# Entry of the softmax attention: expert weight loads on the sync queue, constants filled in the second pipeline step, only some cells cleared

## The chip, the cores and the metric

The kernel runs on one core of a Trainium2 chip, in one launch. The core has five engines with their own instruction streams: TensorE (PE: matmuls, and PEld: its weight loads), VectorE (DVE), ScalarE (ACT), GpSimd (POOL) and SyncE (SP). [...] The metric is the device time of the launch in microseconds (us); lower is better. Before the change the three timed runs gave 1829.85, 1832.07 and 1848.2 us, a median of 1832.07 us.

## The reference, cut to what matters

A network of two layers works on 16 sequences of 256 tokens with 128 channels, float32. Each half layer is `x = x + f(layernorm(x))`:

```python
x = x + _L0_attn_ref(_layernorm(x), ...)   # linear recurrence
x = x + _L0_ffn_ref(_layernorm(x), ...)    # 32 experts, 4 per token
x = x + _L1_attn_ref(_layernorm(x), ...)   # squared-relu attention, 16 heads
x = x + _L1_ffn_ref(_layernorm(x), ...)    # softmax attention, then 8 experts, 1 per token
```

The change lies at the start of the last line. There `_L1_ffn_ref` computes

```python
hn = _layernorm(x, ln1_g, ln1_b)
q, k, v = hn @ wq + bq, hn @ wk + bk, hn @ wv + bv      # 16 heads of 8
attn = softmax(q k^T / sqrt(8)); x = x + (attn @ v @ wo + bo)
hn2 = _layernorm(x, ln2_g, ln2_b)
idx = argmax(hn2 @ gate_w + gate_b)                     # one of 8 experts
x = x + (relu(hn2 @ w1[idx] + b1[idx]) @ w2[idx] + b2[idx])
```

The weights `w1` and `w2` of the 8 experts (2 MB each) are what the change loads from another queue.

## The kernel before, in words

Every engine has its own program, written out by hand; the order of the work is the order of the lines, and engines meet only at semaphores. The program has five stages one after another: the recurrence (with the routing of the first experts), the 32 experts, the squared-relu attention, the softmax attention, and the 8 experts. Between the third and the fourth stage all engines meet at the semaphore `phases`, and SP and another engine clear semaphores for reuse (`cleared`). A printed order gives a reused semaphore the name of an earlier holder, so `x2T_made` in the rows of the change below is `set4`.

The fourth stage works sequence by sequence in a software pipeline of six parts, called `fetch`, `front`, `mid`, `att`, `tail` and `end`. In step n of the pipeline `fetch` treats sequence n+1, `front` sequence n, `mid` sequence n-1, and so on, so step 0 has only `fetch`, and step 1 has `fetch` of sequence 2 and `front` of sequence 1. The first nine steps are written out, then comes a loop. In each step every engine runs its own function `half`:

- `fetch`: SP loads the sequence's rows (`x3l`, 128 KB). DVE takes their moments (L1839 to L1842, `var4`), POOL turns them into an inverse deviation in some small steps (L714 to L755) and makes `x3n` (L756, L757), DVE makes `xn4` (L1845, L1846), PE transposes it (L1440), and ACT brings it from PSUM as `h4T` (L1024).
- `front`: PE multiplies `h4T` by the weights of q, k and v (L1398), DVE adds the biases and writes `v4` and `qk4` (L1875, L1877), and ACT and DVE split q and k into bf16 parts in the tile `terms4`. Its layout is 8 rows of 8 cells a head (`TERMS1`, `DH`); rows 0 to 5 are written in every step, cell 0 of row 6 is a maximum or the constant 1, and the other cells of rows 6 and 7 stay 0.
- `mid`, `att`, `tail`, `end`: the maxima of the scores, softmax and values, output projection with the next layernorm, and routing.

Before the pipeline starts, POOL sets the constants of the stage with memsets, which all add to the semaphore `set4`: `no_token` (L697), all of `terms4` and `v4` (two and four buffers), eight buffers `got` of the last stage, one row of `prior_b`, and then the ones in `terms4` and `v4` (L707, L709). DVE, ACT and PE each wait for all of them before their first instruction of the stage. ACT then starts five transfers, before its own `half`: the clearing of the table `token_dram` in memory, and the last stage's expert weights and biases `wa`, `wb`, `ba`, `bb` (L967, L970). `wa` and `wb` are 2 MB each. SP has the queue for the loads of `x3l` (L535), which it may run four sequences ahead: the load of sequence 5 waits for `kept_made` of sequence 1.

After the pipeline POOL waits for the last entries of the table to have landed, and for DVE's plan of the blocks (`plan_made`), then gathers the table's rows (L791) and the tokens of each block into `got` (L775).

Of the kernel before, what the change touches and what calls it, by code (L numbers as in the profile page):

```python
# [18 lines left out]
P = 128  # L19
# [12 lines left out]
DH = 8  # L32
# [6 lines left out]
AHEAD = 8  # L39
# [36 lines left out]
def pipeline(eng, half, stages=4, unroll=2):  # L76

    def step(turn, at):  # L80
        work = [Seq(turn, at - lag, unroll) if not isinstance(turn, int) or 0 <= at - lag < BATCH else None
                for lag in range(stages)]
        half(*work)


    lead = stages - 1
    turns = (BATCH - lead) // unroll
    for at in range(lead + unroll):
        step(0, at)
    with eng.Fori(1, turns) as turn:  # L90
        for place in range(unroll):
            step(turn, lead + place)
    for at in range(lead + unroll * turns, BATCH + lead):
        step(0, at)
# [20 lines left out]
def build_program(nc, a, out):  # L115
    with ExitStack() as ctx:
# [32 lines left out]
        token_dram = dram("token_dram", (NO_ROWS + P, 1), U32)  # L149
# [104 lines left out]
        s = {}  # L254
# [82 lines left out]
        for name in ("x2_made qk_squared qk_copied v_squared v_copied "  # L337
# [1 line left out]
                     "score_ps relu_made attn_made attn_made_pool attn_made_act attn_read aggr_out aggr_sq_made nsq_ps o_norm_made o_len_made "  # L339
                     "o_tanh_made o_factor_made fT_ps fT_made F_ps gated o_made y3_ps x3_made yg_cleared phases cleared").split():  # L340
            s[name] = sem(name)
        N_SET = 14 + AHEAD
        ring = [bank[6], bank[7]]
        G_BANK = (0, 0, 1, 1)
        FT_BANK = (1, 0)
# [23 lines left out]
        v4 = four("v4", [P, 2, HEADS, COLS])  # L369
# [75 lines left out]
        def _(sp):  # L445
# [69 lines left out]
            def half(fetch, front, att, tail, end):  # L515
                if fetch:
                    wait(sp, s["x2_made"], fetch.n - 2)
                    sp.dma_start(x1l[fetch.p][:], rows(x1_dram, (fetch.n - 1) * SEQ, SEQ, 2)).then_inc(s["x1l_landed"][fetch.p], 16)
                    sp.dma_start(routel[fetch.p][:], rows(route_dram, (fetch.n - 1) * SEQ, SEQ, 2)).then_inc(s["routel_landed"][fetch.p], 16)
                if end:  # L520
                    sp.wait_ge(s["x3_made"], end.n)
                    sp.dma_start(rows(x3_dram, (end.n - 1) * SEQ, SEQ, 2), x3[end.p][:]).then_inc(s["x3_stored"][end.p], 16)
# [7 lines left out]
                sp.sem_clear(semaphore)  # L530
            sp.sem_inc(s["cleared"], 1)
            def half(fetch, front, mid, att, tail, end):
                if fetch:
                    wait(sp, s["kept_made"], fetch.n - 4)
                    sp.dma_start(x3l[fetch.q][:], rows(x3_dram, (fetch.n - 1) * SEQ, SEQ, 2)).then_inc(s["x3l_landed"][fetch.q], 16)  # L535
                if tail:
                    sp.wait_ge(s["x4n_made"], tail.n)
                    sp.wait_ge(s["sum_made"], tail.n)
                    sp.dma_start(rows(x4n_dram, (tail.n - 1) * SEQ, SEQ, 2), x4n[tail.p][:]).then_inc(s["x4_stored"][tail.p], 16)
# [6 lines left out]
        def _(pool):  # L546
# [148 lines left out]
            no_more = pool.to_reg(NO_ROWS - 1)  # L695
            last_token = pool.to_reg(TOK - 1)
            pool.memset(no_token[:], TOK).then_inc(s["set4"], 1)  # L697
            for p in range(2):
                pool.memset(terms4[p][:], 0.0).then_inc(s["set4"], 1)
            for p in range(4):  # L700
                pool.memset(v4[p][:], 0.0).then_inc(s["set4"], 1)
            for n in range(AHEAD):
                pool.memset(got[n][:], 0.0).then_inc(s["set4"], 1)
            pool.memset(prior_b[:, 0:1, :], 0.0).then_inc(s["set4"], 1)
            pool.wait_ge(s["set4"], 8 + AHEAD)
            for p in range(2):
                pool.memset(terms4[p][:, 1, :, :, 6, 0:1].rearrange("q j h a -> q (j h) a"), 1.0).then_inc(s["set4"], 1)  # L707
            for p in range(4):
                pool.memset(v4[p][:, :, :, DH:DH + 1], 1.0).then_inc(s["set4"], 1)  # L709
            pool.wait_ge(s["set4"], N_SET)  # L710

            def inverse_deviation(var, meanvar_x, veps_x, rstd_x, done, count):
                hold(s[var], count)
# [2 lines left out]
                pool.tensor_tensor(rstd_x[:], veps_x[:], minus_half[:, 0:2], ALU.pow).then_inc(s[done], 1)  # L716

            def half(fetch, front, mid, att, tail, end):
                if att:
                    if not isinstance(att.n, int) or att.n > 2:  # L720
                        hold(s["x4_made"], att.n - 2)
                    if not isinstance(att.n, int) or att.n > 2:
                        hold(s["sum_made"], att.n - 2)
                    pool.tensor_copy(x3_plain[att.p][:], x3l[att.q][:]).then_inc(s["plain_made"], 1)
                    hold(s["x3n_made"], att.n)
                    pool.tensor_tensor(x3_kept[att.p][:], x3n[att.q][:], b_o[:].unsqueeze(1).to_broadcast([P, 2, D]), ALU.add).then_inc(s["kept_made"], 1)
                if tail:
                    inverse_deviation("var5", meanvar5, veps5, rstd5, "rstd5", tail.n)
                if end:
                    hold(s["slot1_made"], end.n)  # L730
                    pool.wait_ge(s["table_cleared"], 16)
                    for j in range(2):
                        pool.indirect_dma_start(
                            token_dram, bass.IndirectOffsetOnAxis(ap=slot_b[end.p][:, j:j + 1], axis=0),
                            token[end.p][:, j:j + 1], None, bounds_check=no_more, oob_is_err=False,
                        ).then_inc(s["token_sent"][end.p], 16)
                if tail:
                    if not isinstance(tail.k, int) or tail.k > 1:
                        hold(s["x4_stored"][tail.p], 16 * (tail.k - 1))
                    hold(s["plain_made"], tail.n)  # L740
                    pool.tensor_tensor(x4n[tail.p][:, :, 0:D], x4[tail.p][:], x3_plain[tail.p][:], ALU.add).then_inc(s["sum_made"], 1)
                if fetch:


                    inverse_deviation("var4", meanvar4, veps4, rstd4_in, "rstd4_in", fetch.n)
                    hold(s["rstd4_in"], fetch.n)
                    n = chain.step(pool.tensor_tensor(veps4[:], rstd4_in[:], rstd4_in[:], ALU.mult))
                    chain.need(n)
                    n = chain.step(pool.tensor_tensor(veps4[:], veps4[:], meanvar4[:, :, 1], ALU.mult))
                    chain.need(n)  # L750
                    n = chain.step(pool.tensor_scalar(veps4[:], veps4[:], 1.0, LN_EPS, ALU.mult, ALU.add))
                    chain.need(n)
                    n = chain.step(pool.tensor_tensor(rstd4_norm[:], veps4[:], minus_half[:, 0:2], ALU.pow))
                    chain.need(n)
                    pool.tensor_tensor(rstd4[:], rstd4_norm[:], rstd4_in[:], ALU.mult).then_inc(s["rstd4"], 1)  # L755
                    chain.step(pool.tensor_scalar(x3n[fetch.q][:, 0, :], x3l[fetch.q][:, 0, :], meanvar4[:, 0, 0:1], rstd4_in[:, 0:1], ALU.subtract, ALU.mult))  # L756
                    pool.tensor_scalar(x3n[fetch.q][:, 1, :], x3l[fetch.q][:, 1, :], meanvar4[:, 1, 0:1], rstd4_in[:, 1:2], ALU.subtract, ALU.mult).then_inc(s["x3n_made"], 1)  # L757
                if fetch or tail:
                    chain.restart()

            pipeline(pool, half, 6, 4)
            for p in range(2):
                pool.wait_ge(s["x4_stored"][p], 16 * BATCH // 2)

            def rows_for(dst, turn, q):

# [43 lines left out]
        def _(act):  # L810
# [151 lines left out]
            act.wait_ge(s["phases"], 10)  # L962
            act.wait_ge(s["cleared"], 2)
            act.wait_ge(weights_in, 16 * N_WEIGHT_DMA)
            act.wait_ge(s["set4"], N_SET)

            act.dma_start(token_dram.rearrange("(q n) a -> q (n a)", q=P), no_token[:]).then_inc(s["table_cleared"], 16)  # L967
            for dst, src in ((wa[:], a["wa"].rearrange("e q f -> q e f")), (wb[:], a["wb"].rearrange("e (c q) d -> q (e c) d", q=P)),
                             (ba[:], a["ba"]), (bb[:], a["bb"])):
                act.dma_start(dst, src).then_inc(s["experts_in"], 16)  # L970

            def exp(att, head):
                wait(act, s["pv_made"], HEADS * (att.n - 1) + head + 1 - 4)
# [11 lines left out]
                act.activation(dst[:, 4 * c:4 * c + 4, :].rearrange("q a t -> q (a t)"), ring[x].bitcast(BF16), ACT.Copy).then_inc(s[what + "_out"], 1)  # L985

            def half(fetch, front, mid, att, tail, end):
                flat = terms4[front.p][:].rearrange("q w j h m d -> q (w j h) m d") if front else None
                qk_flat = qk4[:].rearrange("q w j (h d) -> q (w j h) d", d=DH)
                for g in range(PAIRS):  # L990
# [63 lines left out]
        def _(pe):  # L1054
# [241 lines left out]
            pe.drain().then_inc(s["phases"], 1)  # L1296
            pe.wait_ge(s["phases"], 10)
            pe.wait_ge(s["cleared"], 2)
            pe.wait_ge(s["set4"], N_SET)
            readers = [[], []]  # L1300
            LAST_USER = (15, 13, 14)

# [63 lines left out]
                mm.then_inc(s[what + "_ps"], 1)  # L1366

            def half(fetch, front, mid, att, tail, end):

                if end:  # L1370
                    readers[0] = [(s["h5T_made"], end.n)]
# [116 lines left out]
        def _(dve):  # L1488
# [340 lines left out]
            dve.wait_ge(s["phases"], 10)  # L1829
            dve.wait_ge(s["cleared"], 2)  # L1830
            dve.wait_ge(weights_in, 16 * N_WEIGHT_DMA)
            dve.wait_ge(s["set4"], N_SET)
            n = chain.step(dve.tensor_copy(token_f[:], token_start[:]))
            chain.need(n)
            chain.restart()
# [28 lines left out]
                    dve.tensor_reduce(heads[:, :, jp, :], psum[:, 4:6, :].rearrange("q a (b k) -> q a b k", b=2), AX, ALU.max, negate=True).then_inc(s["max_made"], 1)  # L1864

            def half(fetch, front, mid, att, tail, end):
                for g in range(PAIRS):
                    if mid:
                        take_maxima(mid, g)
# [233 lines left out]
```

## Time and profile before

| | us |
|---|---|
| median of the 3 runs shown | 1832.07 |
| the profiled execution | 1849.76 |
| its span on the core | 1848.1 |
| PE / DVE / ACT / POOL busy | 1281.9 / 1097.8 / 755.9 / 902.4 |
| last piece of the third stage (DVE `x3`, L1807) starts | 1178.12 |
| first instruction of the fourth stage (SP, load of `x3l`) | 1180.94 |

The profile's page is of one execution on the chip; times inside it count from its first instruction. A timeline row gives start, duration, engine, line of the kernel, operation, tiles and how many of them (x4), and in square brackets how long the engine had been idle and what released it. Queues (ACTq, SPq, POOLq) are the instruction streams that start transfers: their duration is that of the issue and not of the transfer. In tables by stretch PEclk is TensorE's granted clock as a share of full speed: 0.50 is 1.2 GHz, and 1.00 is 2.4 GHz. The DMA share is the mean busy share of the 16 DMA engines.

### The profile page before, as it was taken

How to read it: one execution, taken by the hardware profiler on the slowest of the kernel's cores; microseconds unless marked ns; L12 is line 12 of the kernel's file. 1: busy time of each engine (PE TensorE's matmuls, PEld its weight loads, DVE VectorE, ACT ScalarE, POOL GpSimd, SP SyncE). 2: the span in 40 equal slices, each digit the busy share in tenths (PEclk: the TensorE clock that was granted, in tenths of full speed). 3: DMA queues.
4: the chain of work that ended last, by engine and by line, in shares of the span. 5: the costliest groups of instructions: out<-in, count | busy, mean ns of one | idle time of the engine just before them, and what ended most of it. 6: DMA issues, size and time to landing. Idle time of an engine off the chain costs nothing. (4 is left out here: it accounts for less than half of the span.)

```text
span 1848.1 us, 26758 instructions
## 1 busy us (share of the span) xinstructions
PE 1281.9 (69%) x8186; PEld 770.1 (42%) x8187; DVE 1097.8 (59%) x2712; ACT 755.9 (41%) x1238; POOL 902.4 (49%) x1119
## 2 busy tenths in 40 slices
PE   3434331636788888888788888348888887847796
PEld 1222221413455555545455555324443443426685
DVE  7777771156666666666666653157787777743232
ACT  1101100315555555555555554026666665632221
POOL 2355567543566666666566644512332332225554
PEclk7555555667788888789788777559999988978766
DMA  4000001700000000000000000120000000001110
GB/s 135 22 15 26 14 2 37 143 16 5 2 8 8 7 7 8 7 7 7 8 7 7 4 4 4 43 72 10 18 11 18 18 18 10 13 19 46 40 42 11
DMA packets 73600, 41.61 MB, mean 23 GB/s; under 512 B 23979, under 2 KB 68908, under 8 KB 73476
## 3 DMA queue, kind: packets, MB, share of 16 engines
q1 hardware_dynamic: 50674, 24.02, 4.8%
q0 software_dynamic: 20432, 11.70, 3.1%
q10 hardware_dynamic: 2370, 4.35, 0.8%
q8 instruction: 65, 1.06, 0.3%
q14 instruction: 59, 0.48, 0.1%
HBM read 31.16 MB, written 23.87 MB: 30 GB/s over the span
## 5 line engine op out<-in xcount | busy, mean ns | idle before, releaser
L1864 DVE TENSOR_REDUCE terms<-psum 128x4 bf16<-128x1024 f32 x128 | 156.9, 1226 | 47.4 <-PE psum L1356 36.9
L1173 PE MATMUL psum<-attn,v 128*64 128x256 f32 x1024 | 163.9, 448 | 1.6 <-ACT aggT L886 1.6
L862 ACT ACTIVATE attn<-psum 128x1024 f32<-128x1024 f32 x128 | 130.5, 1019 | 81.7 <-PE psum L1160 81.5
L632 POOL TENSOR_TENSOR o_inv<-o_norm,minus_half 128x16 f32<-128x16 f32 x32 | 93.3, 2917 | 136.6 <-DVE o_norm L1688 136.6
L975 ACT ACTIVATE prob<-psum 128x512 f32<-128x512 f32 x256 | 138.7, 596 | 38.4 <-PE psum L1320 37.8
L623 POOL DMA_INDIRECT yg<-ye_dram,routel x128 | 131.6, 1028 | 45.1 <-issue 39.0
L714 POOL TENSOR_SCALAR veps<-meanvar 128x2 f32<-128x2 f32 x32 | 6.2, 193 | 294.5 <-DVE meanvar L1842 293.5
L576 POOL DMA_INDIRECT xe_dram<-rows_out,route x128 | 130.4, 1019 | 39.7 <-issue 39.1
L1333 PE MATMUL psum<-prob,v 128*32 128x256 f32 x1024 | 144.6, 406 | 0.7 <-ACT pvT L980 0.4
L1189 PE MATMUL psum<-x3T,w_g 128*128 128x256 f32 x256 | 77.7, 431 | 35.0 <-DVE silu_g L1702 20.1
L1683 DVE TENSOR_TENSOR attn<-psum,attn 128x1024 f32<-128x1024 f32 x80 | 97.0, 1212 | 6.1 <-ACT attn L862 3.1
L1173 PEld LDWEIGHTS psum<-attn,v 128*64 128x64 f32 x1024 | 69.6, 153 | 70.3 <-issue 35.6
L1253 PE MATMUL psum<-w_out,oT 128*128 128x128 f32 x512 | 87.0, 349 | 3.5 <-POOL oT L656 3.5
L1253 PEld LDWEIGHTS psum<-w_out,oT 128*128 128x128 f32 x512 | 84.0, 261 | 8.3 <-issue 8.3
L876 ACT ACTIVATE tanh_g<-psum 128x512 f32<-128x512 f32 x64 | 38.0, 593 | 114.1 <-PE psum L1189 114.1
L1198 PEld LDWEIGHTS psum<-pair_sum,agg_sq 128*128 128x128 f32 x512 | 77.1, 235 | 9.6 <-DVE kT L1713 6.9
L1160 PE MATMUL psum<-qT,kT 64*128 64x256 f16 x512 | 56.9, 305 | 33.1 <-DVE attn L1683 29.0
L1198 PE MATMUL psum<-pair_sum,agg_sq 128*128 128x2 f32 x512 | 77.2, 281 | 2.8 <-DVE kT L1713 1.9
L1356 PE MATMUL psum<-k_highT,q_highT 32*128 32x256 bf16 x512 | 53.9, 291 | 36.4 <-DVE terms L1864 35.5
L656 POOL TENSOR_TENSOR oT<-gate,aggT 128x1024 f32<-128x1024 f32 x32 | 75.5, 2358 | 5.6 <-remote 4.3
L1189 PEld LDWEIGHTS psum<-x3T,w_g 128*128 128x128 f32 x256 | 48.5, 205 | 68.4 <-issue 34.6
L1223 PE MATMUL psum<-ident,terms 128*128 128x128 f16 x512 | 54.1, 280 | 31.9 <-DVEq L1760 31.2
(308 smaller groups left out, 3050.7 us busy)
## 6 DMA issues: line engine op xcount, KB each, us to landing
x4n_dram<-x4n SPq DMA_DIRECT2D x16, 256.0 KB
w<-in_w POOLq DMA_DIRECT2D x48, 64.0 KB, 2.6
x_in<-in_x SPq DMA_DIRECT2D x8, 256.0 KB, 2.7
xe_dram<-zero_rows SPq DMA_DIRECT2D x8, 256.0 KB, 3.0
x_dram<-x1s SPq DMA_DIRECT2D x8, 256.0 KB
xe_dram<-rows_out,route POOLq DMA_INDIRECT x128
xe<-xe_dram SPq DMA_DIRECT2D x16, 128.0 KB
ye_dram<-ye SPq DMA_DIRECT2D x16, 128.0 KB, 2.2
```

Of the source, the lines that this page charges most:

```text
L576: pool.indirect_dma_start(xe_dram, bass.IndirectOffsetOnAxis(ap=where[:, j, K0 + k:K0 + k + 1], axis=0), rows_out[p][:, j, :], None, bound ...
L623: pool.indirect_dma_start(yg[fetch.p][:, j, k, :], None, ye_dram, bass.IndirectOffsetOnAxis(ap=where[:, j, K0 + k:K0 + k + 1], axis=0), bo ...
L632: n = chain.step(pool.tensor_tensor(o_inv[:], o_norm[:], minus_half[:].rearrange("q (j h) -> q j h", j=2), ALU.pow))
L862: act.activation(r[:], psum[:, 2 * (g % 2):2 * (g % 2) + 2, :], ACT.Relu).then_inc(s["relu_made"], 1)
L975: act.activation(prob[head % 4][:], bank[head % 3][:], ACT.Exp, scale=SCALE).then_inc(s["exp_made"], 1)
L1173: mm = pe.matmul(bank[4 + g % 4 // 2][DV * h:DV * h + DV, g % 2 * SEQ:(g % 2 + 1) * SEQ], v[q.p][:, c, head * DV:(head + 1) * DV], attn[g ...
L1189: mm = pe.matmul(b[:, c * SEQ:(c + 1) * SEQ], w_g[:, (2 * u + c) * P:(2 * u + c + 1) * P], x3T[:], start=True, stop=True)
L1198: mm = pe.matmul(b[:, HALF * j + 2 * c:HALF * j + 2 * c + 2], agg_sq[:, c, j * P:(j + 1) * P], pair_sum[:], start=True, stop=True)
L1253: mm = pe.matmul(b[:, j * D:(j + 1) * D], oT[:, c, j * P:(j + 1) * P], w_out[:, c, :], start=(c == 0), stop=(c == PAIRS - 1))
L1333: mm = pe.matmul(bank[3][part, t * SEQ:(t + 1) * SEQ], v4[q.q][:, c, head, :], prob[head % 4][:, c * SEQ:(c + 1) * SEQ], start=(c == 0), s ...
L1683: dve.tensor_tensor(r[:], psum[:, 2 * (g % 2):2 * (g % 2) + 2, :], r[:], ALU.mult).then_inc(s["attn_made"], 1)
L1864: dve.tensor_reduce(heads[:, :, jp, :], psum[:, 4:6, :].rearrange("q a (b k) -> q a b k", b=2), AX, ALU.max, negate=True).then_inc(s["max_ ...
```

## The change: what it does

Four edits, all about the entry of the fourth stage:

1. The transfers of `token_dram` and of the four expert tensors are issued by SP instead of ACT: the table is cleared ahead of the load of sequence 2, as soon as `no_token` is set, and the weights and biases go out ahead of the load of sequence 5.
2. POOL sets only `no_token` before the pipeline. The memsets of `v4`, `terms4` and `prior_b` and the ones stand at the start of POOL's second step.
3. DVE, ACT and PE wait for `set4` at the start of their second step instead of ahead of the first.
4. Of `terms4` only rows 6 and 7 of each head are cleared (128x1024 cells instead of 128x4096, in each of the two buffers), and `got` is cleared after the pipeline, with a wait of POOL for it in front of the last stage.

```diff
@@ SP
             def half(fetch, front, mid, att, tail, end):
+                if fetch and isinstance(fetch.n, int) and fetch.n == 5:
+                    for dst, src in ((wa[:], a["wa"].rearrange("e q f -> q e f")), (wb[:], a["wb"].rearrange("e (c q) d -> q (e c) d", q=P)),
+                                     (ba[:], a["ba"]), (bb[:], a["bb"])):
+                        sp.dma_start(dst, src).then_inc(s["experts_in"], 16)
+                if fetch and isinstance(fetch.n, int) and fetch.n == 2:
+                    sp.wait_ge(s["set4"], 1)
+                    sp.dma_start(token_dram.rearrange("(q n) a -> q (n a)", q=P), no_token[:]).then_inc(s["table_cleared"], 16)
                 if fetch:
                     wait(sp, s["kept_made"], fetch.n - 4)
@@ POOL
             pool.memset(no_token[:], TOK).then_inc(s["set4"], 1)
-            for p in range(2):
-                pool.memset(terms4[p][:], 0.0).then_inc(s["set4"], 1)
-            for p in range(4):
-                pool.memset(v4[p][:], 0.0).then_inc(s["set4"], 1)
-            for n in range(AHEAD):
-                pool.memset(got[n][:], 0.0).then_inc(s["set4"], 1)
-            pool.memset(prior_b[:, 0:1, :], 0.0).then_inc(s["set4"], 1)
-            pool.wait_ge(s["set4"], 8 + AHEAD)
...
+            def set_constant_parts():
+                for p in range(4):
+                    pool.memset(v4[p][:], 0.0).then_inc(s["set4"], 1)
+                for p in range(2):
+                    pool.memset(terms4[p][:, :, :, :, 6:8, :].rearrange("q w j h m d -> q (w j h) (m d)"), 0.0).then_inc(s["set4"], 1)
+                pool.memset(prior_b[:, 0:1, :], 0.0).then_inc(s["set4"], 1)
+                pool.wait_ge(s["set4"], 8)
...
+                pool.wait_ge(s["set4"], N_SET)
...
             def half(fetch, front, mid, att, tail, end):
+                if front and isinstance(front.n, int) and front.n == 1:
+                    set_constant_parts()
...
             pipeline(pool, half, 6, 4)
+            for n in range(AHEAD):
+                pool.memset(got[n][:], 0.0).then_inc(s["set4"], 1)
             for p in range(2):
                 pool.wait_ge(s["x4_stored"][p], 16 * BATCH // 2)
+            pool.wait_ge(s["set4"], N_SET + AHEAD)
@@ ACT (the same wait moves on PE and DVE)
-            act.wait_ge(s["set4"], N_SET)
-
-            act.dma_start(token_dram.rearrange("(q n) a -> q (n a)", q=P), no_token[:]).then_inc(s["table_cleared"], 16)
-            for dst, src in ((wa[:], a["wa"].rearrange("e q f -> q e f")), (wb[:], a["wb"].rearrange("e (c q) d -> q (e c) d", q=P)),
-                             (ba[:], a["ba"]), (bb[:], a["bb"])):
-                act.dma_start(dst, src).then_inc(s["experts_in"], 16)
...
             def half(fetch, front, mid, att, tail, end):
+                if front and isinstance(front.n, int) and front.n == 1:
+                    act.wait_ge(s["set4"], N_SET)
```

The order on POOL, from the end of the third stage, before the change:

```order
L656 TENSOR_TENSOR oT<-gate,aggT 128x1024 [waits gated,y3_ps]
L63 ISA [waits pool_chain]
L697 MEMSET no_token 128x257 [waits cleared,phases]
L699 MEMSET terms 128x4096 x2
L701 MEMSET v 128x1024 x4
L703 MEMSET got 128x256 x8
L704 MEMSET prior_b 128x8
L707 MEMSET terms 128x32 [waits x2T_made]
L707 MEMSET terms 128x32
L709 MEMSET v 128x32 x4
L714 TENSOR_SCALAR veps<-meanvar 128x2 [waits x2T_made,var4]
L716 TENSOR_TENSOR rstd_in<-veps,minus_half 128x2 [waits pool_chain]
```

And in the changed kernel, up to the same place in step 1:

```order
L704 MEMSET no_token 128x257 [waits cleared,phases]
L722 TENSOR_SCALAR veps<-meanvar 128x2 [waits var4]
...
L766 TENSOR_SCALAR x3n<-x3l,meanvar,rstd_in 128x128
L767 TENSOR_SCALAR x3n<-x3l,meanvar,rstd_in 128x128
L63 ISA [waits pool_chain]
L709 MEMSET v 128x1024 x4
L711 MEMSET terms 128x64x16 x2
L712 MEMSET prior_b 128x8
L715 MEMSET terms 128x32 [waits x2T_made]
L715 MEMSET terms 128x32
L717 MEMSET v 128x32 x4
L722 TENSOR_SCALAR veps<-meanvar 128x2 [waits x2T_made,var4]
```

The whole `fetch` of sequence 1 now stands between `no_token` and the other memsets, `got` has left this place, and the memsets of `terms4` are narrower.

SP's queue at the entry of the stage, in the changed kernel (before, the four loads of `x3l` stood there alone, and the next one waited for `kept_made`):

```order
L542 DMA x3l<-x_dram 128x2x128
L539 DMA token_dram<-no_token 128x257 [waits x2T_made]
L542 DMA x3l<-x_dram 128x2x128 x3
L536 DMA wa<-in_wa 128x8x512
L536 DMA wb<-in_wb 128x32x128
L536 DMA ba<-in_ba 128x32
L536 DMA bb<-in_bb 1x1024
L542 DMA x3l<-x_dram 128x2x128 [waits kept_made]
```

The five transfers stand between loads of `x3l`, all of them ahead of the first one that waits for the pipeline.

## Rows read from the trace of the kernel before

**Rows 1.** Timeline of POOL at the entry: start, duration, engine, line, operation [idle before]

```profile
1181.13 0.31 POOL L697 MEMSET no_token<- 128x257 uint32 x1 [9.35 <-SPq L530]
1181.38 6.96 POOL L699 MEMSET terms<- 128x4096 bf16 x2
1188.28 3.64 POOL L701 MEMSET v<- 128x1024 f32 x4
1191.86 2.10 POOL L703 MEMSET got<- 128x256 f32 x8
...
1194.17 0.48 POOL L709 MEMSET v<- 128x32 f32 x4
...
1199.88 0.78 POOL L757 TENSOR_SCALAR x3n<-x3l,meanvar,rstd_in 128x128 f32<-128x128 f32 x1
```

**Rows 2.** Timeline of ACT and its queue, same stretch, same columns

```profile
1194.76 0.37 ACTq L967 DMA_DIRECT2D token_dram<-no_token  x1
...
1196.81 11.56 ACTq L970 DMA_DIRECT2D ba<-in_ba  x1
...
1209.00 0.56 ACT L1024 ACTIVATE h4T<-psum,norms 128x256 f32<-128x256 f32 x1 [13.11 <-issue]
```

**Rows 3.** Timeline of DVE and PE, same stretch, same columns

```profile
1195.16 0.49 DVE L1839 BATCH_NORM_STATS2 stats<-x3l 128x6 f32<-128x128 f32 x2 [0.20 <-DVE token_f L1833]
...
1199.51 0.45 DVE L1846 TENSOR_SCALAR xn<-x3l,meanvar,rstd 128x128 f32<-128x128 f32 x1
...
1200.11 0.66 PE L1440 MATMUL psum<-ident,xn 128*128 128x128 f32 x2 [22.08 <-DVE xn L1846]
...
1209.71 2.90 PE L1398 MATMUL psum<-w_qkv,h4T 128*128 128x384 f32 x4 [8.94 <-ACT h4T L1024]
```

**Rows 4.** Transfers by issue: tiles, count, KB each, median us from issue to landing

```profile
x1l<-x_dram SPq DMA_DIRECT2D x16, 128.0 KB, 2.2
```

**Rows 5.** Timeline of SP's queue: the first loads, and that of sequence 5

```profile
1180.94 62.59 SPq L535 DMA_DIRECT2D x3l<-x_dram  x5
...
1243.15 0.37 SPq L535 DMA_DIRECT2D x3l<-x_dram  x1
```

**Rows 6.** Stretches of 2 us: length, ACT busy (x), PEclk, DMA share, GB/s

```profile
1183.00:1185.00 2.00, 0.00 (x0) 0.50 0.55 147
...
1201.00:1203.00 2.00, 0.00 (x0) 0.50 1.05 402
...
1209.00:1211.00 2.00, 0.56 (x1) 0.50 1.03 279
```

**Rows 7.** The page's DMA queues: packets, MB, share of 16 engines

```profile
q8 instruction: 65, 1.06, 0.3%
```

**Rows 8.** Timeline of POOL and DVE between pipeline and last stage

```profile
1653.21 0.97 POOL L733 DMA_INDIRECT token_dram<-token,slot_b  x1 [0.30 <-issue]
...
1657.63 0.15 DVE L1996 TENSOR_SCALAR block_at_i<-block_at 128x1 uint32<-128x1 f32 x1
1660.95 1.05 POOL L791 DMA_INDIRECT block_tokens<-token_dram,block_at_i  x1 [6.77 <-DMA token_dram<-token,slot_b]
```

**Rows 9.** Stretches of 5 us: length, PE busy (x), PEclk, DMA share, GB/s

```profile
1140.00:1145.00 5.00, 5.00 (x27) 0.50 0.01 2
...
1235.00:1240.00 5.00, 4.13 (x34) 0.50 0.02 3
1240.00:1245.00 5.00, 4.49 (x22) 0.50 0.09 26
1245.00:1250.00 5.00, 4.84 (x46) 1.00 0.00 0
```

**Rows 10.** POOL's first instruction of two steps in the loop

```profile
1329.57 0.19 POOL L714 TENSOR_SCALAR veps<-meanvar 128x2 f32<-128x2 f32 x1 [14.77 <-DVE meanvar L1842]
1354.30 0.19 POOL L714 TENSOR_SCALAR veps<-meanvar 128x2 f32<-128x2 f32 x1 [14.58 <-DVE meanvar L1842]
```

**Rows 11.** A stretch of 50 us: length, PE, PEld, DVE, ACT, POOL busy (x), PEclk, DMA share, GB/s

```profile
1400.00:1450.00 50.00, 41.68 (x388) 19.97 (x384) 39.60 (x112) 32.84 (x57) 17.63 (x32) 1.00 0.08 17
```

More of the change, by code:

```diff
@@ L341, in build_program @@
             s[name] = sem(name)
-        N_SET = 14 + AHEAD
+        N_SET = 14
         ring = [bank[6], bank[7]]
@@ L697, in _ @@
             pool.memset(no_token[:], TOK).then_inc(s["set4"], 1)
-            for p in range(2):
-                pool.memset(terms4[p][:], 0.0).then_inc(s["set4"], 1)
-            for p in range(4):
-                pool.memset(v4[p][:], 0.0).then_inc(s["set4"], 1)
-            for n in range(AHEAD):
-                pool.memset(got[n][:], 0.0).then_inc(s["set4"], 1)
-            pool.memset(prior_b[:, 0:1, :], 0.0).then_inc(s["set4"], 1)
-            pool.wait_ge(s["set4"], 8 + AHEAD)
[L706 to L710, printed above, removed]
+            def set_constant_parts():
[5 more added lines that the diff above has]
+                pool.wait_ge(s["set4"], 8)
+                for p in range(2):
+                    pool.memset(terms4[p][:, 1, :, :, 6, 0:1].rearrange("q j h a -> q (j h) a"), 1.0).then_inc(s["set4"], 1)
+                for p in range(4):
+                    pool.memset(v4[p][:, :, :, DH:DH + 1], 1.0).then_inc(s["set4"], 1)
+                pool.wait_ge(s["set4"], N_SET)
             def inverse_deviation(var, meanvar_x, veps_x, rstd_x, done, count):
@@ L1298, in _ @@
             pe.wait_ge(s["cleared"], 2)
-            pe.wait_ge(s["set4"], N_SET)
             readers = [[], []]
@@ L1368, in half @@
             def half(fetch, front, mid, att, tail, end):
+                if front and isinstance(front.n, int) and front.n == 1:
+                    pe.wait_ge(s["set4"], N_SET)
                 if end:
@@ L1831, in _ @@
             dve.wait_ge(weights_in, 16 * N_WEIGHT_DMA)
-            dve.wait_ge(s["set4"], N_SET)
             n = chain.step(dve.tensor_copy(token_f[:], token_start[:]))
@@ L1866, in half @@
             def half(fetch, front, mid, att, tail, end):
+                if front and isinstance(front.n, int) and front.n == 1:
+                    dve.wait_ge(s["set4"], N_SET)
                 for g in range(PAIRS):
```

## The prediction

> **What bounds the kernel now.** The change touches one place, so I read the profile from that place outward, not from the busy shares. First the timelines of all engines from the end of the third stage to the first steps of the fourth. SP issues the first load of `x3l` at 1180.94 us [rows 5], and TensorE's first multiplication of a sequence's `front` starts at 1209.71 [rows 3]. In these 28.8 us TensorE does two transposes. So this stretch is pure entry, and whatever shortens it moves all that follows, if nothing behind it is bound by something that stays where it is.
>
> Two blocks fill it. POOL sets constants from 1181.13 to 1194.65 (start of the first memset; 1194.17 + 0.48, end of the last) [rows 1], and DVE takes its first moments only then, at 1195.16 [rows 3], although the rows it reads have long been there: a load of this size lands 2.2 us after its issue [rows 4], and the traffic of the four first loads is seen up to 1185 [rows 6]. Then `fetch` of sequence 1 runs quickly, and its transposes end at 1200.77 (1200.11 + 0.66) [rows 3]. But ACT copies them only at 1209.00: its queue had been held for 11.56 us in the issue of the small load `ba`, which stands behind the 4 MB of `wa` and `wb` [rows 2], while the DMA engines were full (share 1.05) from about 1195 to 1211 [rows 6]. That second block costs 8.1 us, from 1200.9 to 1209.0.
>
> **The change, part by part.** All against the profiled execution.
>
> *Waits moved to step 1, memsets behind `fetch` of sequence 1.* DVE can start when `x3l` lands, 1180.94 + 2.2 = 1183.1; with the semaphore about 1183.2. POOL is free then: `no_token` takes 0.31 us [rows 1]. From DVE's first moments to POOL's last `x3n` took 1200.66 - 1195.16 = 5.50 us (1199.88 + 0.78 is the end) [rows 1, 3], so POOL starts its memsets at 1188.7. The same stretch gives the transposes: 1200.77 - 1195.16 = 5.6 us, so they end at 1188.8.
>
> *The weights leave ACT.* ACT is then free for `h4T` at 1188.9, and 0.7 us later (1209.00 to 1209.71 [rows 2, 3]) TensorE could multiply, at 1189.6. At SP the same hold of 11.6 us is free of charge: behind it stands the load of sequence 5, which waited for `kept_made` until 1243.15 in any case [rows 5]; about 15 us earlier that is 1228, and SP would be free near 1198. The loads of sequences 2 to 4 are issued ahead of the weights; only the small clearing of the table (issue 0.37 us [rows 2]) stands between them and the first.
>
> Here a rule speaks against this edit. The row shows an issue of 11.56 us on the queue of a busy engine [rows 2]. The Trainium skill (DMA: Bandwidth & Descriptors, "Issuing engines are not separate DMA queues") says that the queues of all engines end on the same 16 DMA engines, so that another issuing engine saves only the time of the initiation, usually small beside the transfer. By it the edit would bring next to nothing, and the sum would be 8.1 us smaller, 6.7. The trace agrees with the sharing and disagrees with "small", and I go by the row.
>
> *The memsets that are left.* `v4` 3.6 us (1188.28 to 1191.86); `terms4` a quarter of the cells, 6.96 / 4 = 1.74 us; `prior_b` and the ones, from the end of `got` to the end of the last, 1194.65 - 1193.96 = 0.7 us, with the wait between them [rows 1]. Together 6.1 us. No row shows a memset of 128x64x16 cells in strides. It could not cost less than its cells, and I bound it above by the whole tile's 6.96 us, 5.2 more than I take. I take the cells, since `terms4` (4096 cells in 3.48 us) and `v4` (1024 in 0.9) agree on 0.85 ns a cell whatever the tile. So `set4` is complete at 1188.7 + 6.1 = 1194.8, and TensorE starts at 1194.9. This is 5.3 us later than 1189.6: **POOL's memsets, not the matmul's input, end last in the new entry.** The wait is at the head of step 1 on DVE, ACT and PE; nothing else is queued behind it that could have run, since step 1 begins with `front`, and the loads go on by themselves.
>
> *`got` cleared at the end.* 2.1 us [rows 1], between the last scatter of the table's entries (ends 1654.18) and the gather at 1660.95. POOL idles 6.77 us there, waiting for the scatter to land, and DVE's plan is ready at 1657.8 [rows 8]. So it costs nothing; were the landing itself held up by it, 2.1 us.
>
> *Three waits and the order elsewhere*: no price. The `fetch` of sequence 2 hangs on DVE in step 1, and everything from there on is shifted as a block.
>
> Sum: 1209.71 - 1194.9 = **14.8 us** less. The profiled execution would go from 1849.76 to 1835.0 us. It lies 17.7 us above the median of the runs shown, so against that median, 1832.07 - 14.8 = **1817.3 us**, a ratio of 0.992. The bounds of the sum are 9.6 us (strided memset as dear as the whole tile) and 20.1 us (memsets hidden altogether, 1189.6).
>
> **How far a gain of this size can be told.** The shown times spread over 18 us: two near 1831, one at 1848.2, and the profiled one with 1849.76. Something outside the entry moves this kernel by 1%, more than this change does. I call within 1% what a measurement can't tell from no change.
>
> **The rivals.**
>
> *TensorE's clock rises earlier.* The granted clock is 0.50 (1.2 GHz) all through the entry and steps 1 to 3 and rises at about 1245, after stretches with PE busy 4.13 and 4.49 us of 5 [rows 9]. A shorter gap might let it rise a step or two sooner. The q, k, v multiplication takes 2.90 us at the low level [rows 3]; halved, and with transposes and maxima in proportion, some 5 us could go on top: 1812. Against it: steps 1 and 2 are short of work for TensorE whatever precedes them, and 17 us of idle still stand ahead. The Trainium skill (TensorE: Matmul & The Clock Gate, "HAM oscillation") holds that waits between groups of matmuls send the engine back to its low level, so that each group begins slowly; by it nothing would be gained here, and the time stays 1817. The trace agrees as far as it goes: 0.50 in every sparse stretch. Chance 0.15.
>
> *The new step 1 is held up on the way in*: by a dearer strided memset, or by instructions that arrive late. Instructions come over the same DMA engines (65 transfers in one such queue [rows 7]), the weights now fill these from about 1184 to 1200, and step 1 runs from 1194.9 in the midst of that; before, the engines mostly waited then. If an engine had to wait until the burst ends, that is 5 us, as much as the dear memset: 1822.5. The Trainium skill (Runtime: NRT & Kernel Launch, "Instruction fetch mechanics") says that instruction streams are refilled in blocks by DMA while the present block runs, and mostly hidden; by that the time is the forecast's. Before, nothing is seen to be late in the burst (transposes 0.15 us behind their input [rows 3]). Chance 0.13.
>
> *The clock stays low (slower).* At 1140 TensorE was busy for all of 5 us and still granted only 0.50 [rows 9], so much work does not always bring the high level. In the loop a step takes 24.7 us (1329.57 to 1354.30 [rows 10]) with PE busy 83% at full clock [rows 11]: 20.6 us, which would be 41 at half, so each step at the low level costs up to 16.5 us. The place is steps 3 onward, whose start falls elsewhere in time than before. One such step eats the gain, two end at 1850, 1.0% slower. For it speaks only the spread; against it that the rise came promptly at 1245. Chance 0.08, of which 0.05 slower by over 1%.
>
> *The change doesn't do what it says*: the first `x3l` lands late, because the table or the weights go ahead of it, and the entry stays as it was, 1832. The order has it first on the queue. Chance 0.04.
>
> **Chances and range.** The forecast has 0.60. Its ratio of 0.992 is 3.5 us short of the 1% line at 1813.7, and the spread of runs is larger: I give 0.11 of it to faster by over 1%, 0.01 to slower, 0.48 to within. With the early clock (0.14 faster, 0.01 same), the held-up step (0.13 same), the low clock (0.05 slower, 0.03 same) and no effect (0.04 same): faster 0.25, same 0.69, slower 0.06. The range reaches from 1810 (the bound of 20.1 us less 2 us of spread) to 1836 (a gain of 14.8 us on the upper group of times, 1848.2 to 1849.8, is 1833.4 to 1835.0).
>
> **What would show it.** In the profile of the changed kernel: DVE's first moments about 2.2 us behind SP's first load; the ACT row of `h4T` 5 to 6 us later with no issue on ACTq; POOL's memsets for some 6 us right behind `x3n`, `terms` with 0.87 us each; TensorE's first q, k, v multiplication 14 us after that first load and released by POOL; a long issue of `ba` on SPq that nobody waits for; the gather L791's counterpart still released by the landing of the table's entries; the rise of the clock some 35 us behind the first multiplication, as before. Wrong would be the sum if that multiplication starts at the right place and the time is not lower: then the loss lies in the clock or behind step 1.

## The result

The changed kernel took 1822.7 us in the median of 8 runs, beside 1841.12 us for the kernel before (8 runs, the three shown at the top among them). The ratio is 0.9897, 95% interval 0.9849 to 0.9946: 19 us less, with 10 to 28 us possible. Timed a second time on another occasion it was 0.991 (0.9874 to 0.9945), 1824.07 against 1838.05 us, where the medians alone give 14.0 us and 0.992. Ratios and intervals are estimated from the single runs, without two slow executions of the kernel before, so they differ a little from the quotients of the medians. The entry of the fourth stage became 15.0 us shorter in the profile, where 14.8 had been worked out. That is 0.992 of the whole and lies inside both intervals.

The profiled execution of the changed kernel had a span of 1816.5 us, 31.6 less than before. Only 15.0 us of that lie in the entry, as the stretches show (starts of the same instructions in both profiles; what the other 9.1 and 7.9 us are worth is told with the second profile of the kernel before, below):

| stretch | before | changed | less |
|---|---|---|---|
| start to first load of the second stage | 314.98 | 305.91 | 9.1 |
| second and third stage | 865.96 | 866.18 | -0.2 |
| **entry: SP's first `x3l` to the first q, k, v multiplication** | **28.77** | **13.78** | **15.0** |
| from there to the gather of the table | 451.24 | 443.36 | 7.9 |
| from there to the end | 187.2 | 187.3 | -0.1 |

### The profile page after: what moved, and what is told of

It is laid out like the page before. It is cut to its first block and busy times, and to the rows that moved or that the text cites. A ratio compares the mean times of both kernels' runs of the same rounds, so it can differ in the third digit from the quotient of the medians.

```text
span 1816.5 us, 26759 instructions
## 1 busy us (share of the span) xinstructions
PE 1267.4 (70%) x8186; PEld 758.0 (42%) x8187; DVE 1097.8 (60%) x2712; ACT 756.0 (42%) x1237; POOL 898.0 (49%) x1119
```

## The profile after

The timeline of the changed kernel at the entry, POOL first. The columns are those of [rows 1]; these rows answer to them.

```profile
1172.29 0.31 POOL L704 MEMSET no_token<- 128x257 uint32 x1 [9.37 <-SPq L530]
...
1178.99 0.78 POOL L767 TENSOR_SCALAR x3n<-x3l,meanvar,rstd_in 128x128 f32<-128x128 f32 x1
1179.72 3.61 POOL L709 MEMSET v<- 128x1024 f32 x4
1183.29 1.83 POOL L711 MEMSET terms<- 128x1024 bf16 x2
...
1185.34 0.48 POOL L717 MEMSET v<- 128x32 f32 x4
```

The memsets run one behind the other from 1179.72 to 1185.82, 6.10 us, right behind `x3n`. The two strided ones of `terms4` take 1.83 us together, where the whole tiles took 6.96 [rows 1].

SP's queue and the other engines in the same stretch, which answer to [rows 2, 3, 5]:

```profile
1172.09 0.39 SPq L542 DMA_DIRECT2D x3l<-x_dram  x1
1172.63 0.36 SPq L539 DMA_DIRECT2D token_dram<-no_token  x1
...
1174.26 0.49 DVE L1848 BATCH_NORM_STATS2 stats<-x3l 128x6 f32<-128x128 f32 x2 [1.98 <-DMA x3l<-x_dram]
...
1176.15 11.11 SPq L536 DMA_DIRECT2D ba<-in_ba  x1
...
1179.21 0.66 PE L1450 MATMUL psum<-ident,xn 128*128 128x128 f32 x2 [10.02 <-DVE xn L1855]
...
1179.99 0.56 ACT L1033 ACTIVATE h4T<-psum,norms 128x256 f32<-128x256 f32 x1 [22.54 <-PE psum L1450]
...
1185.87 2.93 PE L1408 MATMUL psum<-w_qkv,h4T 128*128 128x384 f32 x4 [6.00 <-POOL v L717]
```

Read the brackets. DVE's moments are now released by the landing of `x3l`, 2.17 us after its issue, and no longer by a memset. ACT's `h4T` follows the transposes (0.12 us behind their end) and is released by them, where 13.11 us of idle had ended in "issue" [rows 2]. And the multiplication is released by POOL's last memset of `v`, after 6.00 us of idle. The long issue of `ba` is still there with 11.11 us, but on a queue that nobody waits for: SP's next load goes out at 1219.38, 32 us after that issue ends.

TensorE's clock, in the form of [rows 9]:

```profile
1185.00:1190.00 5.00, 2.93 (x4) 0.50 1.03 281
...
1215.00:1220.00 5.00, 4.35 (x27) 0.50 0.00 0
1220.00:1225.00 5.00, 4.99 (x32) 0.75 0.09 26
1225.00:1230.00 5.00, 3.81 (x38) 1.00 0.00 0
```

The high level comes at about 1222, 36 us behind the first multiplication; before it was 35 (1245 against 1209.71). The first of these rows also shows the multiplication running inside the burst of the weights (DMA share 1.03): it takes 2.93 us there. Before it took 2.90 [rows 3], in the last 2 us of the burst [rows 6], and in a kernel without a burst at this place (`late_weights`, below) 2.92.

The place of the `got` memsets, in the form of [rows 8]:

```profile
1620.94 0.97 POOL L743 DMA_INDIRECT token_dram<-token,slot_b  x1 [0.30 <-issue]
1621.90 2.10 POOL L773 MEMSET got<- 128x256 f32 x8
1629.23 1.05 POOL L804 DMA_INDIRECT block_tokens<-token_dram,block_at_i  x1 [5.23 <-DMA token_dram<-token,slot_b]
```

POOL still idles behind them, for 5.23 us, until the table's entries have landed.

## Experiments

"Landmark" is the entry as in the table above, 28.77 us before and 13.78 in the changed kernel.

### Edit 1 alone

```diff
@@ kernel before
-            act.dma_start(token_dram..., no_token[:])...
-            for dst, src in ((wa[:], ...), (wb[:], ...), (ba[:], ...), (bb[:], ...)):
-                act.dma_start(dst, src).then_inc(s["experts_in"], 16)
@@ SP, half: as in the change (table ahead of sequence 2, weights ahead of sequence 5)
```

> The kernel before with edit 1 alone: the table's clearing and the expert weights go out on SP, all memsets stay in front as they were. Landmark: from SP's first load of x3l to the start of TensorE's first q, k, v multiplication (28.8 us before, 13.8 in the changed kernel). Theory (ACT's queue was held by the issue behind the 4 MB): h4T follows the transposes at once, the landmark falls by 8.1 to about 20.7 us, the time by 8 us. Rival (by the Trainium skill, DMA: Bandwidth & Descriptors, "Issuing engines are not separate DMA queues", only the initiation is saved): landmark 28, time unchanged. Second rival (the transfer itself, not its issue, held ACT's first copy up): landmark 28 too.

Measured: landmark 20.65 us, ratio 0.9938 (0.9912 to 0.9964). Its timeline:

```profile
1174.55 0.39 SPq L542 DMA_DIRECT2D x3l<-x_dram  x1
...
1178.61 10.95 SPq L536 DMA_DIRECT2D ba<-in_ba  x1
...
1194.49 0.56 ACT L1027 ACTIVATE h4T<-psum,norms 128x256 f32<-128x256 f32 x1 [34.58 <-PE psum L1443]
1195.20 2.90 PE L1401 MATMUL psum<-w_qkv,h4T 128*128 128x384 f32 x4 [0.83 <-ACT h4T L1027]
```

`h4T` is released by the transposes, and the landmark falls by 8.1 us as expected; the interval of the ratio leaves out the rival's "time unchanged". The transfers are the same; what went is ACT's hold in the issue. The second rival, that the transfer itself held up ACT's first copy, isn't refuted by this run alone, since here the DMA engines had fallen idle by 1193, ahead of `h4T`. The changed kernel refutes it: its `h4T` at 1179.99 runs in the middle of the burst (DMA share 1.05 from 1180 to 1185) and follows the transposes by 0.12 us. So what the Trainium skill (DMA: Bandwidth & Descriptors, "Issuing engines are not separate DMA queues") says, that another issuing engine saves only the initiation, holds; its "usually small" does not hold behind 4 MB, where the issue takes 11 to 12 us.

### Everything but edit 1

```diff
@@ changed kernel, SP: the five dma_start taken out again
@@ ACT
             act.wait_ge(weights_in, 16 * N_WEIGHT_DMA)
+            act.wait_ge(s["set4"], 1)
+            act.dma_start(token_dram..., no_token[:])...    # and wa, wb, ba, bb as before
```

> The changed kernel with edit 1 undone: memsets moved, narrowed and split as in the change, but ACT still issues the table's clearing (after no_token) and the four expert tensors ahead of its first step. If the edits added up, this would be worth 15.0 - 8.1 = 6.9 us: landmark 21.9. Theory (the two blocks overlap once the memsets are out of the way, each hides most of the other): ACT's hold runs from about 1 us to 14 us after SP's first load, h4T starts near 14.3, multiplication near 15: landmark 15, time 13.8 us below before. So edit 1 would be worth only about 1.2 us of the changed kernel.

Measured: landmark 16.42 us, ratio 0.9919 (0.9882 to 0.9955).

```profile
1168.40 2.00 SPq L535 DMA_DIRECT2D x3l<-x_dram  x4
...
1171.06 12.42 ACTq L976 DMA_DIRECT2D ba<-in_ba  x1
...
1181.64 0.48 POOL L710 MEMSET v<- 128x32 f32 x4
...
1184.11 0.56 ACT L1032 ACTIVATE h4T<-psum,norms 128x256 f32<-128x256 f32 x1 [13.97 <-issue]
1184.82 2.90 PE L1407 MATMUL psum<-w_qkv,h4T 128*128 128x384 f32 x4 [8.64 <-ACT h4T L1032]
```

The theory of overlap holds: edits 2 to 4 alone bring 12.35 us and not 6.9, since ACT's hold now runs while `x3l` lands, `fetch` is worked on and POOL clears. I was 1.4 us short: the issue of `ba` ends 15.1 us after the first load, not 14 (it took 12.42 us here). So edit 1 is worth 8.1 us on the old entry and 2.6 us (16.42 - 13.78) on the new one, where I had expected 1.2.

### The whole of `terms4` cleared

```diff
@@ changed kernel, POOL
-                    pool.memset(terms4[p][:, :, :, :, 6:8, :].rearrange(...), 0.0)
+                    pool.memset(terms4[p][:], 0.0)
```

> The changed kernel with the whole of terms4 cleared (128x4096 cells in each of two buffers instead of 128x1024). Theory (POOL's memsets end last in the new entry): they take 5.2 us longer (6.96 instead of 1.83 us), and the landmark grows by the same, from 13.8 to 18.9. Rival (the matmul's input or the weights' transfer ends last): landmark stays below 15.

Measured, in a single run: landmark 18.77 us.

```profile
1186.06 6.96 POOL L711 MEMSET terms<- 128x4096 bf16 x2
...
1193.77 2.93 PE L1408 MATMUL psum<-w_qkv,h4T 128*128 128x384 f32 x4 [11.12 <-POOL v L717]
```

The memsets took 5.13 us longer and the multiplication started 4.99 us later, with the same releaser. POOL's memsets are what ends last. Without the narrowing the change would have taken 10.0 us from the entry (28.77 to 18.77), with it 15.0.

### The memsets split once more

```diff
@@ changed kernel, POOL: step 0, ahead of the first moments
+                if not front and fetch:
+                    set_first_parts()      # v4[0], terms4[0], prior_b and their ones
@@ POOL: step 1
-                    set_constant_parts()
+                    set_other_parts()      # v4[1..3], terms4[1], got and their ones
@@ PE, ACT, DVE
-                if front and isinstance(front.n, int) and front.n == 1:
-                    pe.wait_ge(s["set4"], N_SET)
+                if front and isinstance(front.n, int) and front.n < 3:
+                    pe.wait_ge(s["set4"], 6 if front.n == 1 else N_SET + AHEAD)
```

> The changed kernel with the memsets split again: what step 1 reads (v4, terms4 of sequence 1, prior_b) is set ahead of the first moments, while x3l lands and POOL idles 2.6 us; the other three v4, the other terms4 and got are set in step 1 and waited for in step 2. Theory (POOL's memsets end last, the input only 5.3 us earlier): the landmark falls from 13.8 to 8.5 us, the time by another 5.3 us, to 20 us below before; and with got out of the place after the pipeline, the table's entries land about 0.5 us earlier after the last scatter (7.3 us in the changed kernel, 6.8 before). Rival (something else is just behind, as the weights' transfer): landmark 12 or more.

Measured: landmark 8.57 us, ratio 0.9862 (0.9825 to 0.9899).

```profile
1175.96 0.95 POOL L711 MEMSET terms<- 128x1024 bf16 x1
1176.76 0.49 DVE L1864 BATCH_NORM_STATS2 stats<-x3l 128x6 f32<-128x128 f32 x2 [1.95 <-DMA x3l<-x_dram]
...
1177.73 0.19 POOL L739 TENSOR_SCALAR veps<-meanvar 128x2 f32<-128x2 f32 x1 [0.42 <-DVE meanvar L1867]
...
1182.48 0.56 ACT L1049 ACTIVATE h4T<-psum,norms 128x256 f32<-128x256 f32 x1 [22.50 <-PE psum L1466]
...
1183.19 2.90 PE L1424 MATMUL psum<-w_qkv,h4T 128*128 128x384 f32 x4 [0.83 <-POOL v L709]
```

The first memsets, 1024 cells of `v4` and of `terms4` and the small ones, fit into the time in which `x3l` lands, and POOL still waits 0.42 us for the moments. The multiplication starts 0.71 us after `h4T`, as before in [rows 2, 3]. The releaser named there, a memset of `v`, had not been on the way: it belongs to the count that is waited for one step later. The second expectation failed in part: from the start of the table's last scatter to the gather it took 8.21 us, against 8.29 with `got` in between. With `got` in that place five profiles gave 7.94 to 8.29 us; without it seven gave 7.72 to 8.64, two of them of the kernel before. The memsets there cost nothing that shows.

### The kernel before against itself

> The kernel before, unchanged, against itself, to see how much of the measured difference can be chance. Every kernel timed so far came out 3 to 5 us further below before than its entry is shorter (w_only 11.4 against 8.1, m_only 14.9 against 12.4, the changed kernel 18.9 against 15.0, early_fills 25.4 against 20.2). In the profiles the first load of the second stage (xe) starts at 314.98 us before and at 305 to 306 in all five others, though the first stage's code is the same. Theory (chance, of the first stage's own): ratio within 0.3% of 1, and xe at either value. Rival (something of the program before slows its first stage in every execution): xe near 315 again, and a first stage that costs the changed kernel's lead some us which the change's description doesn't hold.

Measured: ratio 0.999 (0.9955 to 1.0025). The first load of the second stage starts at 305.88 us, and the landmark is 28.66.

```profile
1165.14 1.93 SPq L535 DMA_DIRECT2D x3l<-x_dram  x4
...
1193.80 2.90 PE L1398 MATMUL psum<-w_qkv,h4T 128*128 128x384 f32 x4 [8.84 <-ACT h4T L1024]
```

So the 9.1 us of the first stage in the table above are chance of one execution (the other eleven profiles have 304.2 to 306.2 us there), and the landmark repeats within 0.1 us. Of the 7.9 us between the entry and the gather most is chance too: this second profile of the kernel before takes 445.04 us there, the first took 451.24, and the ten profiles of changed kernels 440.3 to 445.3. The ratio's interval, 0.35% to either side, says how much chance can do in the times: 6 us. The third stage shows where most of the spread of the times is: the stretch from 365 us to the first `x3l`, in this execution and in the first one of the changed kernel (length, busy time of PE, PEld, DVE, ACT and POOL, PEclk, DMA share, GB/s):

```profile
365.00:1165.14 800.14, 628.44 (x3744) 377.62 (x3744) 496.35 (x992) 404.78 (x544) 458.79 (x445) 0.83 0.03 7
```

```profile
365.00:1172.09 807.09, 640.60 (x3744) 384.06 (x3744) 496.83 (x992) 405.50 (x544) 456.82 (x444) 0.81 0.03 7
```

The busy times of DVE and ACT agree to 0.2%; the length goes with TensorE's granted clock. Over the twelve profiles of this study it was 800 to 824 us at mean clocks of 0.83 down to 0.78, in a stage that no kernel here changes.

### The weights four steps later

```diff
@@ changed kernel, SP
-                if fetch and isinstance(fetch.n, int) and fetch.n == 5:
+                if fetch and isinstance(fetch.n, int) and fetch.n == 9:
```

> The changed kernel with the four expert tensors issued by SP ahead of the load of sequence 9 instead of 5, so that the entry runs without their 4 MB on the DMA engines. Theory (the transfer doesn't hold up the new step 1): landmark from SP's first load to the first q, k, v multiplication 13.8 us as in the changed kernel, and from there to the first store of x4n 76.4 us within 1. Rival (step 1 is held up by the burst, through late instructions or data): both together shorter by 2 us or more.

Measured, in a single run: landmark 13.85 us, and 74.95 us from there to the first store of `x4n` (76.44 in the changed kernel).

```profile
1182.10 0.39 SPq L542 DMA_DIRECT2D x3l<-x_dram  x1
...
1195.95 2.92 PE L1408 MATMUL psum<-w_qkv,h4T 128*128 128x384 f32 x4 [6.01 <-POOL v L717]
```

```profile
1195.00:1200.00 5.00, 2.92 (x4) 0.50 0.00 0
```

The DMA engines are idle now (share 0.00), and the landmark and the multiplication are as with the burst. The second stretch is 1.5 us shorter, outside the "within 1" of the theory and short of the rival's 2 us. But a second profile of the changed kernel (below), with the burst in its place, shows 74.95 too, and `early_fills`, whose first multiplication starts some 9 us before its burst ends, took 76.31 and 73.17 in its two profiles. So this stretch moves by more than 1.5 us from one execution to the next, and nothing shows that the burst holds up step 1.

### TensorE kept busy through the entry

```diff
@@ early_fills, PE
+            def keep_busy(count):
+                for _ in range(count):
+                    pe.matmul(bank[2][:, 0:P], before[:], ident_b[:], start=True, stop=True)
+            keep_busy(70)
...
+                    if front and not att and isinstance(front.n, int):
+                        keep_busy((20 if g == 0 else 80 if g == 2 else 0) if front.n == 1 else 10)
```

> early_fills with extra bf16 matmuls 128x128 on TensorE, whose result nobody reads (70 ahead of the first transposes of the stage, 80 + 20 in step 1, 10 in each eighth of step 2), to keep it busy through the entry. This prices the rival of the earlier clock. Theory (the low clock of steps 1 to 3 costs a few us, and work brings the high level): granted clock 1.00 from step 1 on, and from the first q, k, v multiplication to the first store of x4n about 71 us instead of 76.3; time 5 us below early_fills. Rival (the steps are bound by DVE and ACT, so the clock is worth nothing there, or the extra matmuls don't raise it): 76 us or more.

Measured: from the first multiplication to the first store 71.37 us, against 76.31 in `early_fills`; ratio 0.9897 (0.9849 to 0.9945).

```profile
1170.63 6.88 PE L1330 MATMUL psum<-ident_b,before 128*128 128x128 bf16 x70 [2.97 <-SPq L530]
...
1178.74 1.53 PE L1431 MATMUL psum<-w_qkv,h4T 128*128 128x384 f32 x4 [0.83 <-ACT h4T L1049]
```

```profile
1175.00:1180.00 5.00, 4.17 (x37) 0.84 0.92 303
1180.00:1185.00 5.00, 4.59 (x79) 1.00 1.05 330
1185.00:1190.00 5.00, 1.64 (x30) 1.00 0.78 213
```

The clock rises inside the entry, the q, k, v multiplication takes 1.53 instead of 2.90 us, and 4.9 us go from the profile. But the high level doesn't stay, as the theory had it. After the last row, in which TensorE was busy for 1.64 of 5 us, it is gone again, and the multiplication of sequence 2 takes its 2.90 us:

```profile
1190.00:1195.00 5.00, 4.29 (x14) 0.52 0.00 0
```

```profile
1191.91 2.90 PE L1431 MATMUL psum<-w_qkv,h4T 128*128 128x384 f32 x4 [0.21 <-ACT h4T L1049]
```

In the times the gain wasn't to be seen (`early_fills` had 0.9862), so three kernels were timed once more side by side.

### Three kernels side by side

The changed kernel, `early_fills` and `warm`, each unchanged, on one chip.

> The changed kernel again, beside early_fills and warm on one chip, for times that can be compared. Theory (the entry alone: 15.0 us of 1835 to 1840, the 3 to 4 us on top in the first timing were chance): ratio 0.992 within its interval, landmark 13.8, third stage anywhere from 808 to 826 us with the granted clock of TensorE there. Rival (a lead beyond the entry): ratio 0.989 or lower again.

> early_fills again. Theory: 20.2 us of entry less than before, ratio 0.989, 5 us below the changed kernel; landmark 8.6.

> warm again (in its first profile the stretch from the first q, k, v multiplication to the first store of x4n was 71.4 us, against 74.9 to 76.7 in all others). Theory (the high clock in the first steps is worth 3.5 to 5 us and costs nothing elsewhere): ratio 0.987, some 4 us below early_fills. Rival (the extra matmuls are paid for later by a lower clock): as early_fills or above it.

| | median us | ratio to before (95%) | landmark | to the first store |
|---|---|---|---|---|
| before | 1838.05 | 1 | 28.7 | 75.7 and 75.8 |
| changed | 1824.07 | 0.991 (0.9874 to 0.9945) | 13.77 | 74.95 |
| early_fills | 1816.49 | 0.9883 (0.9847 to 0.9919) | 9.38 | 73.17 |
| warm | 1817.9 | 0.9878 (0.9839 to 0.9916) | 8.16 | 71.35 |

(The line of the kernel before has its medians here and its stretches from its two profiles.) The changed kernel's ratio is 0.991, between the theory's 0.992 and the rival's 0.989, and its interval holds both; it decides neither way. In `early_fills` `x3l` landed 0.8 us later this time, which is all of the longer landmark. `warm` shortens the first steps in both of its profiles, by 1.8 to 5 us, but its time can't be told from that of `early_fills`. Neither of its expectations for the time is shown. Both are faster than the kernel before; that they beat the changed one by their 4 to 6 us of entry is in the profiles, and in the medians for `early_fills` in both of its timings, but inside the intervals.

## Why the prediction was right

It named 1817.3 us against a median of 1832.07, a ratio of 0.992; measured 0.9897 and 0.991. The measured time of 1822.7 us lies in its range. That it is 5 us above the forecast comes of two differences that partly cancel: the kernel before has 1841.12 us over 8 runs, 9 us more than the three runs gave, and the medians fell by 18.4 us, 3.6 more than the 14.8 forecast. What is right about the forecast is the entry; that the time landed this near to it is in part luck.

- *Two blocks in the entry, memsets and ACT's hold*: right. Each was taken away alone; the landmark fell from 28.77 to 20.65 without the hold and to 16.42 with the memsets moved and narrowed.
- *POOL's memsets end last in the new entry, 5.3 us behind the input*: right. The bracket says so, `full_terms` moved the start with them, and `early_fills` took out the 5.2 us (13.78 to 8.57).
- *Their size, 6.1 us*: 6.10. The strided memset costs its cells, 0.89 us from one start to the next against 0.87 worked out; the bound of the whole tile was far off.
- *DVE's start 2.2 us behind the load*: 2.17; it varied to 2.9 once.
- *The hold is free on SP, and as long there*: right, 11.11 us with 32 us to spare.
- *`got` is free after the pipeline*: right, and its alternative price of 2.1 us isn't there.
- *The weights' burst*: the rival of 0.13, late instructions or a dear memset in step 1, did not come. By the Trainium skill (Runtime: NRT & Kernel Launch, "Instruction fetch mechanics") refills are mostly hidden, and the trace agrees: 2.93 us for the multiplication in the burst, 2.92 without one in `late_weights`.
- *The earlier clock*: it did not come in the changed kernel, whose level rose 36 us behind the first multiplication, much as before. The Trainium skill (TensorE: Matmul & The Clock Gate, "HAM oscillation") has waits send TensorE back to its low level, and the traces agree: 0.50 from 1175 to 1220, and in `warm` a fall to 0.52 behind the stretch with 1.64 of 5 us busy. With other entries the level did rise early for some us and fell back (mean 0.69 from 1185 to 1190 in `m_only`, 0.84 from 1200 to 1205 in `early_fills`), so that this rival was nearer than "steps 1 and 2 are short of work" made it. Its price of some 5 us is shown as to size only: with work added for it, `warm` gained 4.9 us in its first pair of profiles and 1.8 in its second.
- *The low clock as a danger*: not of the entry. But what I left as "something outside the entry" has a place now: the third stage, 800 to 824 us at mean granted clocks of 0.83 down to 0.78.
- *The rule on issuing engines*: `w_only` refuted that edit 1 brings next to nothing. But my price of this rival was wrong: I took the 8.1 us that ACT's hold costs in the old entry off the sum for the new one and got 6.7. `m_only` is the kernel in question, and it gained 12.35 us. The parts don't add: 8.1 and 12.35 us alone, 15.0 together, since the hold mostly runs beside `fetch` and the memsets once these have moved. The forecast itself was not touched by this, since it followed the whole new entry and not the edits one by one.

My chances put 0.69 on "within 1%", and the two ratios are 1.03% and 0.9%, on either side of the line. The few us beyond 15.0 in the first timing were not there in the medians of the second (14.0); both intervals hold 15.0, and behind the entry the profiles differ by no more than executions of one kernel do. Whether any of it is real stays open.

## What to carry to other kernels

Look at what an engine does between a stage's barrier and its first useful instruction: constants for later steps can go behind the first step's loads, and into the time in which these land. Don't leave a small load behind megabytes on the queue of an engine that computes; put it where the next transfer isn't due for long. And where two such blocks run in parallel, price them on the entry that is left, and look for the one that ends last: it says what the next edit should be.

## What the runs showed of the hardware

The issue of a small load behind 4 MB on the same queue took 10.95 to 12.42 us in the entry on ACT's queue and on SP's alike, and 14.89 us in `late_weights` beside the pipeline's traffic, while the issues around it took 0.3 to 0.9 us. A memset on POOL took, from one start to the next, 0.85 to 0.89 ns for each cell of a partition in tiles of 1024 and 4096 cells, for f32 and bf16 and in strides of 16 cells of 64 alike; in the tiles `got` of 256 cells it was 1.0 ns (2.10 us for eight). And 70 small matmuls without a use brought TensorE's clock from 1.2 to 2.4 GHz ahead of the stage's first real multiplication, with the landmark at 8.18 us against 8.57 without them; the clock was back at 1.2 GHz for the next sequence's.
